# TensorE's written-out attention program, aligned to a slot of a program block in every second macro

## What is computed

```python
hs = (x @ Ws + bs).reshape(N, H, HD)            # N 1250, H 8, HD 96
hd = (x @ Wd + bd).reshape(N, H, HD)
hs_e = hs[src]
e = jax.nn.leaky_relu(hs_e + hd[dst], SLOPE)
logits = jnp.einsum('ehd,hd->eh', e, attn)
m = jax.ops.segment_max(logits, dst, num_segments=N)
ex = jnp.exp(logits - m[dst])
s = jax.ops.segment_sum(ex, dst, num_segments=N)
alpha = ex / s[dst]
out = jax.ops.segment_sum(alpha[..., None] * hs_e, dst, num_segments=N)
```

## Time and profile before

| | |
|---|---|
| runs | 2206.68, 2210.77, 2211.57 us; median 2210.77 |
| the profiled execution, its own time | 2215.05 us |
| its span, first to last instruction | 2213.3 us |
| TensorE matmul busy | 2106.6 us |
| VectorE / ScalarE / GpSimd busy | 1674.1 / 1134.5 / 948.1 us |
| mean granted TensorE clock | 0.985 |
| attention of the first layer, first messages to the last shown | 551.30 to 1197.04 us |
| attention of the second layer | 1428.45 to 2066.33 us |

### The profile page before, as it was taken

One profiled execution on the slowest core, in us unless ns is written; L12 is line 12 of the kernel. 1 busy time (PEld: TensorE's weight loads), 2 busy tenths in 40 slices (PEclk: granted clock), 3 DMA queues, 4 the chain that ended last, 5 costly groups with the idle time before them and its releaser, 6 DMA issues. The chain is left out here.

```text
span 2213.3 us, 86039 instructions
## 1 busy us (share of the span) xinstructions
PE 2106.6 (95%) x31007; PEld 1719.3 (78%) x31007; DVE 1674.1 (76%) x4435; ACT 1134.5 (51%) x2749; POOL 948.1 (43%) x849
## 2 busy tenths in 40 slices
PE   7999999998999999999998899899999999999798
PEld 4665555555999989899997555699999999999676
DVE  5545882354988988888898764488899999899884
ACT  1111200024766767666675413466666777677574
POOL 0000001022666666566662311366666667677121
PEclk9999999999999999999999999999999999999899
DMA  5001044144888888788884225488888888888411
GB/s 196 1 0 65 25 134 146 52 131 126 248 254 255 249 255 244 230 253 254 249 260 135 82 88 134 140 250 253 254 246 259 260 251 260 251 258 254 178 73 49
DMA packets 143396, 404.03 MB, mean 183 GB/s; under 512 B 21811, under 2 KB 81625, under 8 KB 143073
## 3 DMA queue, kind: packets, MB, share of 16 engines
q0 software_dynamic: 59584, 298.64, 44.7%
q1 hardware_dynamic: 79691, 93.00, 13.3%
q10 hardware_dynamic: 3828, 7.85, 1.1%
HBM read 370.77 MB, written 17.17 MB: 175 GB/s over the span
## 5 line engine op out<-in xcount | busy, mean ns | idle before, releaser
L502 ACT ACTIVATE at_relu<-at_turned,ah_attn_size 128x512 f32<-128x512 f32 x1092 | 712.2, 689 | 393.0 <-PE at_turned L565 384.5
L483 POOL DMA_INDIRECT at_rows<-table,ah_index x360 | 428.5, 1190 | 234.0 <-DVE ah_index L702 108.0
L483 POOL DMA_INDIRECT ah_room<-table,ah_index x352 | 428.1, 1216 | 210.4 <-DVE ah_index L702 116.7
L692 DVE SCALAR_TENSOR_TENSOR sums<-sums,at_factor,at_total 128x97 f32 x1456 | 360.4, 309 | 32.0 <-issue 19.0
L559 PE MATMUL at_turned<-ident,ah_room 128*128 128x128 f32 x2208 | 345.8, 280 | 22.3 <-PEq L1658 18.8
L559 PE MATMUL at_turned<-ident,at_rows 128*128 128x128 f32 x2160 | 331.6, 276 | 1.2 <-issue 1.0
L559 PEld LDWEIGHTS at_turned<-ident,ah_room 128*128 128x128 f32 x2208 | 246.4, 143 | 45.4 <-issue 45.2
L659 DVE SCALAR_TENSOR_TENSOR at_relu<-at_relu,ah_pair_sign 128x512 f32<-128x512 f32 x364 | 256.1, 745 | 0.0
L559 PEld LDWEIGHTS at_turned<-ident,at_rows 128*128 128x128 f32 x2160 | 236.4, 141 | 21.6 <-issue 21.4
L682 DVE TENSOR_TENSOR at_spread<-at_lined,at_weight 128x1024 f32<-128x1024 f32 x182 | 221.3, 1216 | 17.5 <-ACT at_weight L512 16.8
L565 PE MATMUL at_turned<-ah_place,dst_rows 96*128 96x128 bf16 x2208 | 219.3, 221 | 3.8 <-issue 3.7
(11 more groups left out here) (317 smaller groups left out, 3129.7 us busy)
## 6 DMA issues: line engine op xcount, KB each, us to landing
at_flags<-run_flags SPq DMA_DIRECT2D x182, 64.0 KB
dst_rows<-pr_parts SPq DMA_DIRECT2D x76, 144.0 KB, 2.5
ah_place<-local_rows SPq DMA_DIRECT2D x92, 96.0 KB
at_place<-local_rows SPq DMA_DIRECT2D x90, 96.0 KB
table<-ah_room SPq DMA_DIRECT2D x20, 400.0 KB, 2.4
ah_room<-table,ah_index POOLq DMA_INDIRECT x368
at_rows<-table,ah_index POOLq DMA_INDIRECT x360
mx_w<-in_L_mix_W_qkv SPq DMA_DIRECT2D x4, 1152.0 KB, 12.1
```

The costliest lines, as they stand in the source:

```text
L483: pool.indirect_dma_start(rows[b][:, j, :], None, table, bass.IndirectOffsetOnAxis(index[b][:, j:j + 1], 0)).then_inc(gathered[b], 16)
L502: act.activation(relu[c][:], turned[chunk(b, c)][:], ACT.Relu, scale=attn_size[:, c:c + 1]).then_inc(bent, 1)
L692: dve.scalar_tensor_tensor(into[:, k], into[:, k], factor[b % 2][:, j, k:k + 1], part(j)[:, k, 0:HW], ALU.mult, ALU.add).then_inc(added, 1)
```

## The change

In a slot that has messages, and where the macro that is turned has an even buffer number, TensorE's program is aligned ahead of the sixth chunk (chunk 5): the chunk's first instruction is placed at slot 96 of a program block, and the gap ahead of it is branched over. This holds for macros 2, 4, ... 90 of each layer. Nothing else changes.

```diff
                     if turn:
                         turn_linear(turn[0])
+                        if message and turn[1] % 2 == 0:
+                            pe.addr_align(256, offset=96, max_nops=0)
                         turn_chunk(*turn, at, 5)
                     return following
```

## The result

The changed kernel takes 2357.49 us at the median of 4 runs (2354.53 to 2366.08), the kernel before 2208.72 us (4 runs). The ratio is 1.067, with a 95% interval of 1.0647 to 1.0693. It is slower, as forecast, and inside the range of 2270 to 2590, but the 149 us are half of the 296 that were forecast.

The account below looks back on a forecast made before the run. TensorE was taken to set the time. 90 pairs of macros at 2.25 + 1.5 = 3.75 us add 338, drifting waits take off 41: 2215.05 profiled becomes 2512, less 4.3 for the median, 2507 us; range 2270 to 2590.

Parts of the forecast that it names:

- the rival of the short delay: Packet delay after the sixth chunk's start falls to 1.25 us, wait 1.3 us, clock kept: 2287 us; chance 0.18.
- The bound, the edges, the fetch of one block ahead: TensorE sets the time; it stops at edges of 256-slot program blocks, as only the next block is on order.
- The jump costs nothing, its target is in hand: Branch ahead of the sixth chunk: costed at nothing, sequencer ahead of the array, target in the block already on order.
- The long blocks wait little: A pair's other two blocks, 6.1 and 5.4 us, are close to the 5.6 us block to block: no wait of weight.
- The wait of the short block, 2.25 us: Slots 96 to 255 last 2.3 us, the next block is usable at 4.55: wait 2.25 us per two macros.
- The clock, 1.5 us a pair: After most short-block waits TensorE's clock drops, losing 1.7 us; weighted by 0.87, 1.5 us per two macros.
- The drifting waits go, -41 us: Present waits at block edges drifting through late heads and early chunks all vanish: -41 us.
- The rule of the Trainium skill: Crossing a 16 KiB block costs one queue tail update, mostly hidden; by it the change costs nothing, about 2211 us.

Follow-up runs that it names:

- e12_light_slot224: Changed kernel with the sixth chunk at slot 224 instead of 96 and attention-loop gathers fetching 200 of 800 columns: 2178.2 us, 0.985 of the kernel before.
- e1_slot0: Changed kernel with the sixth chunk at slot 0 instead of 96: 2301.6 us, 1.041 of the kernel before.
- e4_slot224: Changed kernel with the sixth chunk at slot 224 instead of 96: 2351.3 us, 1.065 of the kernel before.
- light gathers: Gathers inside the attention loop fetch 200 of 800 columns of a row: 2175.3 us on the kernel before, 2247.4 us on the changed kernel.
- slot 48: Changed kernel with the sixth chunk at slot 48 instead of 96: 2311.0 us, 1.047 of the kernel before.

## Why the prediction was right in kind and too high in size

The measured 2357 us are below the forecast's own range, 2375 to 2590. They are in the stated range only because that took in the rival of the short delay.

**The bound, the edges, the fetch of one block ahead.** Right. The waits stand at the slot that counting gives, in the change and in every layout tried, and each ends some 2.4 us after its packet starts.

**The jump costs nothing, its target is in hand.** Right: no wait over 0.15 us before the sixth chunk in the change, and 3 us for 90 jumps in e12_light_slot224. That a taken jump can force a fetch, as the Trainium skill ("Runtime: NRT & Kernel Launch", Instruction fetch mechanics) says of a target outside the blocks in hand, no run here shows.

**The long blocks wait little.** Right for slot 96: no wait over 0.15 us at their edges. It was near the limit, as e1_slot0 and e4_slot224 show.

**The wait of the short block, 2.25 us.** Too high by a fifth: 1.79. The packet started 1.67 us after the chunk at the mean (0.6 to 2.7), not 2.2. The prediction held the delay fixed by the phase of the gathers. The light gathers show that it falls with the DMA load, and with the slower period the share fell from 0.83 to 0.77. But the average share is not all of it: behind the waits with slot 48, at 0.79, the next packet took 3.2 us, against 2.3 in the change. So what shortened the delay at this place was not shown. The rival of the short delay had the direction, not the size.

**The clock, 1.5 us a pair.** This is the step that failed: "14 of the 16 delays would give a wait clearly over 1.57, so I add 1.7 x 0.87 = 1.5 us." The price of one fall was right (1.7 us), its frequency wrong: 65 of the 88 waits were over 1.57 us, and the clock fell after 7 of them, all over 2.1 us; that is 0.14 us a pair. Three waits of the kernel before, of 1.57, 1.65 and 2.23 us, had been read as a threshold. There is none at that length: over all runs the clock fell after 5 of 177 waits of 1.5 to 2.0 us, and two of these 5 were of the three. Of the 1.73 us a pair by which the forecast is above the measured 2.02 (178.1 over 88), the clock is 1.36 and the wait 0.46, less 0.1 for the slower matmuls behind each wait.

**The drifting waits go, -41 us.** Right: 40.7 in the same stretches, and none left.

**The rule of the Trainium skill (the same section) that crossing a block is mostly hidden.** It agrees with the light gathers, where the edges of the kernel before cost nothing. It does not hold at the DMA share of this kernel, 0.83, at which its edges cost 33 to 41 us, nor in the change, at 0.77, where they cost 137 us more.

What stays open: what decides after which waits the clock falls, and why an order after a jump takes 3.9 to 4.2 us and after an edge 5.3 to 5.8 under full gathers. A different backlog of gathers at the two places would do it, but this was only argued.

## What to carry to other kernels

A written-out program is itself a stream of transfers: at some 22 ns an instruction a block of 256 lasts 5.5 us here, and a block must last as long as the next one takes to come, which grows with the load of the DMA engines (without lead, 3.9 us at a share of 0.34; at 0.7 to 0.8, 3.9 to 4.2 behind a jump and 5.3 to 5.8 behind an edge). Padding to a fixed slot in every macro or two adds blocks without adding work, so it makes this worse, above all where the block entered holds the densest instructions; count the time of each block, not its slots. And a threshold seen in three events is a guess: give such a term both of its ends in the range and a middle value in the sum.

## What was not expected of the hardware

An order of a block took 3.9 to 4.2 us after a jump and 5.3 to 5.8 after an edge, at about the same share of the DMA (0.69 to 0.79). An empty instruction from the loader held TensorE for at least 0.07 us, three times the average of its own instructions here, so 124 of them cost 8.7 us. And the granted clock fell after only 5 of 177 waits of 1.5 to 2.0 us, but after two in three of those above 2.7.
